# Two output units of a scan-and-matmul kernel summed in two pieces: six tiles' shares in step 24, shelved in SBUF, and joined by VectorE in step 26

## What is computed

```
decay = exp(-exp(w)) * (0.5 + 0.5 * tf)          # tf = sigmoid(sum(time_emb)), one per batch
ek = exp(min(k, 30)); ekv = ek * v               # here k = v = fside
nf, df = forward scans of ekv, ek with decay     # a = a * decay + x, over 1024 times
nb, db = the same, backward
num = nf + nb - ekv + exp(min(u + k, 30)) * v
den = df + db - ek  + exp(min(u + k, 30))
base = sigmoid(x) * num / max(den, 1e-8) * (0.8 + 0.2 * tf)
out = x + base @ (sign(weight) * mean|weight|).T + bias
```

## Time and profile before

| | |
|---|---|
| median of 3 runs | 514.49 us (511.86 to 514.51) |
| the profiled execution's own time | 513.52 us |
| its span in the trace | 511.5 us |
| VectorE busy | 482.0 us (94%) |
| ScalarE, GpSimd, TensorE busy | 413.9 (81%), 380.3 (74%), 352.3 us (69%) |
| mean granted TensorE clock | 0.87 |

### The profile page before, as it was taken

One profiled execution on the slowest core, in us unless ns is written; L12 is line 12 of the kernel. 1 busy time (PEld: TensorE's weight loads), 2 busy tenths in 40 slices (PEclk: granted clock), 3 DMA queues, 4 the chain that ended last, 5 costly groups with the idle time before them and its releaser, 6 DMA issues.

```text
span 511.5 us, 5395 instructions
## 1 busy us (share of the span) xinstructions
PE 352.3 (69%) x1797; PEld 206.7 (40%) x1803; DVE 482.0 (94%) x346; ACT 413.9 (81%) x461; POOL 380.3 (74%) x210
## 2 busy tenths in 40 slices
PE   3323223332194877878597879869739999999996
PEld 2213223332152444335354445535425555544442
DVE  6999999999999699999999999999999999999566
ACT  3979899899979889988987989998797888894500
POOL 0067778748764987789788687889897799899483
PEclk9997666565678798898987989989987999999999
DMA  8878999999987498798979869989792679975379
GB/s 219 220 220 267 263 260 243 307 297 251 246 191 179 68 240 182 163 199 189 195 170 160 201 130 203 197 178 202 162 162 49 118 124 157 178 127 80 42 107 223
DMA packets 101283, 94.22 MB, mean 184 GB/s; under 512 B 2924, under 2 KB 93064, under 8 KB 100744
## 3 DMA queue, kind: packets, MB, share of 16 engines
q0 software_dynamic: 31440, 36.18, 46.9%
q1 hardware_dynamic: 67720, 56.65, 35.7%
q10 hardware_dynamic: 2096, 1.05, 0.8%
HBM read 60.31 MB, written 37.75 MB: 192 GB/s over the span
## 4 chain that ended last, share of the span: by engine, by line
POOL 27%; ACT 25%; PE 21%; issue 18%; DVE 7%; DMA 0%; SPq 0%; ACTq 0%; DVEq 0%; POOLq 0%
POOL wkv L379 11%; PE prod L447 8%; POOL acts L342 5%; POOL out_dram L355 4%; ACT x_nat L801 4%; POOL wkv L385 3%; ACT euk L659 3%; PE prod L488 3%; ACT terms L655 3%; ACT L806 3%; POOL terms L388 2%; ACT L801 2%; ACT rec L690 2%; PE sT L488 2%; PE kT L488 2%
## 5 line engine op out<-in xcount | busy, mean ns | idle before, releaser
L447 PE MATMUL prod<-acts,sgn 128*128 128x512 f16 x752 | 182.7, 399 | 0.0
L925 DVE TENSOR_TENSOR_SCAN terms<-cols,y_start,terms 128x1024 f32<-128x1024 f32 x64 | 147.0, 2337 | 1.1
L911 DVE TENSOR_TENSOR_SCAN terms<-cols,terms 128x1024 f32<-128x1024 f32 x64 | 142.8, 2272 | 0.0
L362 POOL TENSOR_TENSOR wkv<-wkv,terms 128x1024 f32<-128x1024 f32 x31 | 73.5, 2370 | 54.8 <-DVE wkv L954 54.8
L447 PEld LDWEIGHTS prod<-acts,sgn 128*128 128x128 f16 x752 | 77.2, 103 | 88.5 <-issue 16.7
L379 POOL TENSOR_TENSOR wkv<-euk,rec 128x1024 f32<-128x1024 f32 x31 | 82.1, 2648 | 33.2 <-ACT rec L692 33.1
L342 POOL TENSOR_TENSOR acts<-wkv,rec 128x1024 f16<-128x1024 f32 x30 | 78.4, 2612 | 5.0 <-ACT rec L701 4.9
L385 POOL TENSOR_TENSOR wkv<-wkv,rec 128x1024 f32<-128x1024 f32 x31 | 79.6, 2569 | 1.2 <-ACT wkv L753 1.2
L422 PE MATMUL prod<-ident,o_nat 128*128 128x128 f16 x64 | 8.3, 311 | 72.0 <-ACT o_nat L794 72.0
L422 PE MATMUL sT<-ident,x_nat 128*128 128x128 f32 x208 | 36.7, 334 | 27.5 <-ACT x_nat L801 11.2
L422 PE MATMUL kT<-ident,k_nat 128*128 128x128 f32 x248 | 43.4, 333 | 15.9 <-DVE own L942 15.8
(11 more groups left out here) (120 smaller groups left out, 585.7 us busy)
## 6 DMA issues: line engine op xcount, KB each, us to landing
terms<-own POOLq DMA_DIRECT2D x32, 512.0 KB, 5.2
out_dram<-in_x_dram SPq DMA_DIRECT2D x32, 512.0 KB, 7.2
k_nat<-in_fside_BxSxS_dram SPq DMA_DIRECT2D x30, 512.0 KB, 6.4
x_nat<-in_x_dram SPq DMA_DIRECT2D x26, 512.0 KB, 4.9
out_dram<-o_nat POOLq DMA_DIRECT2D x24, 512.0 KB, 8.4
y_fm<-in_L_ffn_weight_dram SPq DMA_DIRECT2D x8, 512.0 KB, 8.4
out_dram<-in_L_ffn_bias_dram POOLq DMA_DIRECT2D x8, 512.0 KB, 6.6
x_end<-in_x_dram SPq DMA_DIRECT2D x6, 512.0 KB, 8.7
```

Of the source, the lines that this page charges most:

```text
L362: pool.tensor_tensor(wkv[n % 2][:, :], wkv[n % 2][:, :], ekv[n % NV], ALU.mult).then_inc(st["base"], 1)
L447: ins = pe.matmul(made_in(u), view[:, c, m % CT * P:m % CT * P + P], acts[:, part, m // CT % 2 * CT + c, h * H:(h + 1) * H], start=(part = ...
L911: dve.tensor_tensor_scan(buf, d, buf, 0.0, ALU.mult, ALU.add).then_inc(st["F" + kind], 1)
L925: dve.tensor_tensor_scan(buf[:, ::-1], d, buf[:, ::-1], y_start[:, i:i + 1], ALU.mult, ALU.add)\
```

## The change

Units 35 and 36 are summed in two pieces. In step 24 TensorE first sums the shares of tiles 16 to 21 of both (12 matmuls each, `begun`); ScalarE empties them with scale and bias onto two shelves in SBUF (`shelve`, at the end of exps(25)), and only then does TensorE start units 33 and 34 in the same banks (`shelved`). In steps 25 and 26 units 35 and 36 take the 4 matmuls of tiles 22 and 23 alone, ScalarE's evac(35) and evac(36) go, and VectorE joins bank and shelf into y_fm, both after `own` of step 26 (`fused`). Besides, in step 25 halves(23) come ahead of inverse(24) on ScalarE, and lo(23) ahead of the store and of chk(24) on GpSimd.

```diff
+    SHELVED = (4 * CT + 3, 4 * CT + 4)
+        shelf = [acts[:, 0, 2 * CT - 2 + i, :].bitcast(F32) for i in range(len(SHELVED))]
# GpSimd, step
                 if low:
                     base(n - 2)
+                if n == LAST + 1:
+                    low_half(n - 2, p)
                 if n < N - 1:
                     for m in ready[0:1]:
                         store(m)
...
-                if low:
+                if low and n != LAST + 1:
                     low_half(n - 2, p)
# TensorE
+            def emptied(u):
+                if u in SHELVED:
+                    pe.wait_ge(st["fused"], SHELVED.index(u) + 1)
+                else:
+                    done(pe, "ev", u - sum(v < u for v in SHELVED))
+            def shelve(u):
+                done(pe, "lo", u // (2 * CT) * CT + CT - 3)
+                product(u, range(CT - 2), 0, CT - 3).then_inc(st["begun"], 1)
             def unit(u):
                 done(pe, "lo", u // (2 * CT) * CT + CT - 1)
-                done(pe, "ev", u - 2)
-                product(u, range(CT)).then_inc(st["prod"], 1)
+                emptied(u - 2)
+                if u in SHELVED:
+                    product(u, range(CT - 2, CT), CT - 2).then_inc(st["prod"], 1)
+                else:
+                    product(u, range(CT)).then_inc(st["prod"], 1)
                 if ahead:
                     turned(made(n) - 1)
-                    for u in (made(n) + 1, made(n) + 2):
+                    for u in SHELVED:
+                        shelve(u)
+                    for i, u in enumerate((made(n) + 1, made(n) + 2)):
+                        pe.wait_ge(st["shelved"], i + 1)
                         part(u, 0, CT - 2)
# ScalarE
+            def shelve(i):
+                m = SHELVED[i] // 2
+                act.wait_ge(st["begun"], i + 1)
+                act.activation(shelf[i], made_in(SHELVED[i]), ACT.Identity, scale=oscale[:, m:m + 1],
+                               bias=bcol[:, m:m + 1]).then_inc(st["shelved"], 1)
             def clear(lo, hi):
                 for u in range(lo, hi):
-                    evac(u)
+                    if u not in SHELVED:
+                        evac(u)
             def step(n, p, wt, nxt, nxt3, mid, low, late):
+                if n == LAST + 1:
+                    done(act, "base", n - 2)
+                    halves(n - 2, p)
                 if mid:
                     inverse(n - 1, 1 - p)
...
-                if low and not hasty:
+                if low and not hasty and n != LAST + 1:
...
                     exps(n + 1, 1 - p)
+                if n == LAST:
+                    for i in range(len(SHELVED)):
+                        shelve(i)
# VectorE, after own(n)
+                if n == LAST + 2:
+                    for i, u in enumerate(SHELVED):
+                        done(dve, "prod", u)
+                        done(dve, "yT", u - 4)
+                        dve.scalar_tensor_tensor(y_fm[u // 2 % 2][:, u % 2 * H:(u % 2 + 1) * H], made_in(u),
+                                                 oscale[:, u // 2:u // 2 + 1], shelf[i], ALU.mult, ALU.add)\
+                           .then_inc(st["fused"], 1)
```

More of the change, by code:

```diff
@@ L183, in bi_wkv_binary_ffn @@
             "ln", "rec", "chk", "two", "inv", "gate", "base", "hi", "hib", "lo",
-            "prod", "ev", "yT", "yc", "abs", "sgn", "wT", "wTc", "orow", "orow_sb", "early", "early_sb", "soon", "nat", "weighed", "joined", "scaled", "whole",
+            "prod", "ev", "yT", "yc", "abs", "sgn", "wT", "wTc", "orow", "orow_sb", "early", "early_sb", "soon", "begun", "shelved", "fused", "nat", "weighed", "joined", "scaled", "whole",
             "res", "prior_hi", "prior_hib", "prior_lo", "last_den", "last_ln", "last_rec", "last_chk", "last_inv", "last_gate",
@@ L440, in s_turn, with product @@
                      ident[:, :]).then_inc(st["sT"], 1)
-            def product(u, tiles):
+            def emptied(u):
[3 more added lines that the diff above has]
+                    done(pe, "ev", u - sum(v < u for v in SHELVED))
+            def product(u, tiles, opens=0, closes=CT - 1):
                 m, h = u // 2, u % 2
@@ L448, in product @@
                                         acts[:, part, m // CT % 2 * CT + c, h * H:(h + 1) * H],
-                                        start=(part == 0 and c == 0), stop=(part == 1 and c == CT - 1))
+                                        start=(part == 0 and c == opens), stop=(part == 1 and c == closes))
                 return ins
+            def shelve(u):
+                done(pe, "lo", u // (2 * CT) * CT + CT - 3)
+                product(u, range(CT - 2), 0, CT - 3).then_inc(st["begun"], 1)
             def part(u, lo, hi):
@@ L464, in unit @@
                 done(pe, "lo", u // (2 * CT) * CT + CT - 1)
-                done(pe, "ev", u - 2)
-                product(u, range(CT)).then_inc(st["prod"], 1)
+                emptied(u - 2)
[3 more added lines that the diff above has]
+                    product(u, range(CT)).then_inc(st["prod"], 1)
             def turned(u):
                 if 0 <= u < 2 * LAST:
-                    done(pe, "ev", u)
+                    emptied(u)
                     done(pe, "yc", u - 1)
@@ L510, in step @@
                 if n == N - 2:
-                    done(pe, "ev", 2 * LAST - 2)
+                    emptied(2 * LAST - 2)
                     begun(0)
@@ L544, in step @@
                 if first and n != LAST + 1:
-                    done(pe, "ev", units[0] - 2)
+                    emptied(units[0] - 2)
                     part(units[0], 0, CT - 1)
@@ L559, in step @@
                 if first and n != LAST + 1:
-                    done(pe, "ev", units[1] - 2)
+                    emptied(units[1] - 2)
                     part(units[1], 0, CT - 1)
```

## The result

| | before | after |
|---|---|---|
| median | 513.73 us (4 runs, 511.86 to 514.51) | 519.59 us (4 runs, 518.74 to 520.86) |
| profiled execution, its span | 513.52 us, 511.5 us | 518.78 us, 516.9 us |

The changed kernel is slower: ratio of the times 1.0122, 95% interval 1.0081 to 1.0162. The forecast was 520.1 us.

The account below looks back on a forecast made before the run. The prediction took VectorE to bound the kernel: 7.9 us of later scans, joins included, less 1.3 us of overlap given back, made 6.6 us on the profiled 513.52, so 520.1 us, with a range of 516.5 to 522.4 us.

Parts of the forecast that it names:

- VectorE bounds: Whole kernel: VectorE, busy 94% of the span, sets the time; the end moves one for one with its shift at gate(28).
- Rival (c): TensorE's backlog from 386 us on sets the end, so 24 fewer matmuls there give 508.3 us; chance 0.06.
- the wait of 0.59 us: Step 30, at 457.04: TensorE's wait for a ScalarE copy ahead of the tail, taken as its backlog's slack of 0.59 us.
- Part 1: The two joins on VectorE: about 0.65 us each, together a cost of 1.3 us.
- Part 2: Shelving in step 24: 24 matmuls, 5.2 us, cost nothing on TensorE; two evacuations put ScalarE 1.3 us later.
- Part 3: Step 25's new order: two(24) 5.1 us later (halves 1.2, lo 2.3, store 1.6); gate(24) waits 2.4 us for inv(24).
- Part 4: Joins' inputs: TensorE idles 6.4 us before turned(32), half clock follows, join 36 waits, step 26's scans begin 7.9 us late.
- Rival (a): Step 25: same mechanism, but TensorE's clock stays up or returns at once; scans 4.9 us late, 517.1 us; chance 0.18.
- Part 5: Step 27: the overlap of inv(26) with den(27) is gone, giving back 1.34 us on VectorE.
- Sum: Whole kernel: 7.9 - 1.3 = 6.6 us on the profiled 513.52, forecast 520.1 us; chance 0.56.

Follow-up runs that it names:

- e4: The kernel before with 24 matmuls (tiles 16 to 21 of units 35 and 36) left out and nothing in their place: 511.37 us, ratio 0.9989.
- e1: The changed kernel with step 25 in its old order, shelving and joins alone: 515.0 us, ratio 1.0051.
- e3: The changed kernel with the store's DMA issue in step 25 back ahead of lo(23): 517.92 us, ratio 1.0104.
- e6: The changed kernel with both joins behind the forward scans of step 26 instead of ahead of them: 515.07 us, ratio 1.005.
- e12: The changed kernel with TensorE repeating tile 24's transposes 5 times ahead of turned(32): 516.34 us, ratio 1.0091.
- e11: The changed kernel with TensorE repeating tile 24's transposes 4 times ahead of turned(32): 516.88 us, ratio 1.0091.
- e10: The changed kernel with TensorE repeating tile 24's transposes 3 times ahead of turned(32): 519.2 us, ratio 1.012.
- e9: The kernel before with two more 128x512 passes on VectorE in step 28, results unused: 513.81 us, ratio 1.0031.
- e5: The changed kernel with TensorE repeating tile 24's transposes 6 times ahead of turned(32): 516.52 us, ratio 1.0079.
- e2: The kernel before with the new order of step 25 alone, no shelving and no joins: 518.06 us, ratio 1.0108.

## Why the prediction was right, point by point

**VectorE bounds, and its shift at step 28 is the shift of the end.** Right for the changed kernel. Between den(28) and the last VectorE instruction lie 79.55 us before and 79.51 after, though TensorE had 24 matmuls less behind it and waits 2.00 us once in step 30. e4, with less work on TensorE alone, keeps the distance as well (79.53). Rival (c) is out: what e4 takes off TensorE doesn't come back at the end. It isn't a law, though: in e1 and e3 the clock fell in step 30, the wait of 0.59 us was used up, and the end came 0.9 us later than VectorE's shift.

**Part 1, joins 1.3 us.** 1.32 in e1, 1.33 in e6.

**Part 2, the shelving.** Right: it is free on TensorE, which waited 1.29 us for the first shelving and still ended its sums at 382.9. On ScalarE the first pass behind the table load starts at 375.91; with the 1.19 us by which den(25) stood earlier in this execution that is 377.1, as forecast, 1.3 us behind the 375.77 of the earlier trace rows. This 1.3 us isn't free: it is a part of the 5.1 us of part 3, and in e1, without the new order, it brings inv(24) beside den(25).

**Part 3.** two(24) stands 0.18 us behind den(25)'s start, before 4.95 ahead of it: 5.13 us later, forecast 5.1. gate(24) waits 2.46, forecast 2.4. The store's share of the 5.1, put at 1.6, is 1.54 by e3.

**Part 4.** TensorE idles 6.49 us (6.4), half clock follows, the scans begin 7.79 us late (7.9). The second join waits 2.85 us, a little less than the 3 to 4 that I gave; the first waits 0.88, which the forecast's own numbers had (own ends at 392.5, join 35 at 393.3) and which costs nothing of its own, as the second waits for the same engine behind it. Rival (a) is the one whose size was off: I priced a clock that stays up at 3.0 us less, e12 and e11 show 2.4. From turned(32) to the end of unit 36 I had walked 3.6 us at the full clock, and the second join came 4.0 us behind it; at half clock I had walked 6.6, and it was 6.46. The walk at the full clock already had the second join waiting 1.05 us (393.15 to 394.2); it waits 1.35.
The Trainium skill, "TensorE: Matmul & The Clock Gate", "What's actually happening", has the clock low when the engine has idled; the changed kernel and e10 agree (0.50 behind breaks of 6.49 and 4.20 us).

**Part 5.** den(27) takes 1.23 us, 1.33 less than in the earlier trace rows, and the loss falls from 7.79 to 6.46. From there to the tail nothing on VectorE waits for over 0.2 us.

**Sum.** Forecast 6.6, found 6.46. The profiled executions differ by 5.26 us only, since den(25) stood 1.19 us earlier in the one after: 6.46 - 1.19 = 5.27. That is scatter and no part of the change: e9, whose code up to step 28 is that of before, has den(25) at 384.89. The medians differ by 5.86. That the time itself came within 0.5 us, 519.59 against 520.1, is in part luck: the four runs of the changed kernel lie 2.1 us apart, and the one execution on which the forecast was built turned out to lie 0.2 us from the median of before.

## What to carry to other kernels

Ask of the engine that seems full whether a wait still stands ahead of the work that sets the end; here it did (0.59 us), and 5.2 us of matmuls moved away from TensorE could bring 1.3 us at most, which the two joins put back on the engine that does bound. Before one instruction goes ahead in an in-order queue, walk everything that it pushes back, DMA issues included, to the bounding engine: 1.2 us of halves that came later, 2.3 us of lo(23) and 1.5 us of a store became 5.1 us at two(24) and, by a second path over an evacuation and TensorE, 6.5 us on VectorE. A consumer placed on the bounding engine costs its wait too, so it goes where its input is long there: behind two scans the same joins cost 3.6 us less.

## What the runs showed beyond that

**TensorE's clock after a break.** The break's length alone doesn't tell whether the clock falls. Ahead of turned(32) 1.33 us (e1), 2.14 (e12) and 3.03 (e11) left it at 1.00, 4.20 (e10), 4.96 (e3) and 6.49 didn't. In step 30, behind the same matmuls, a break of 2.02 us was followed by half clock in e1 and e3; one of 2.02 us in e5 and e10, and one of 2.00 us in the changed kernel, was not. The break and the work behind it, e1 first:

```profile
450.42:452.44 2.02, 0.00 (x0) 0.00 (x1) 1.88 (x3) 1.58 (x3) 2.02 (x2) 1.00 1.33 167
452.44:455.44 3.00, 3.00 (x8) 1.12 (x9) 3.00 (x2) 2.91 (x4) 3.00 (x4) 0.57 0.05 6
```

```profile
456.04:458.04 2.00, 0.00 (x0) 0.00 (x1) 1.86 (x3) 1.58 (x3) 2.00 (x2) 1.00 1.39 175
458.04:462.20 4.16, 3.63 (x16) 1.48 (x16) 4.13 (x3) 4.07 (x6) 4.16 (x4) 1.00 0.06 9
```

e1 and e3 are also the two kernels that need 0.9 us more from den(28) to the end (80.46 and 80.44 against 79.5 in all others): the 8 matmuls behind the break took 3.21 us in e1, 2.98 in e3 and 1.90 in the changed kernel. In e1 the next 15 then begin 29.43 us behind den(28) and without a wait (457.59), in the changed kernel 28.47 us behind it and after the wait of 0.59 (462.26). What decides between the two cases wasn't tried, and stays open; whether the other runs of e1 and e3 had the low clock there isn't known, as one execution of each was profiled.

**VectorE beside GpSimd.** A den that starts while GpSimd's product runs can take longer, and then ends 1.1 us after it: 2.09 us in e1, 3.23 in e3 (inv(24) ends at 388.01, den(25) at 389.10), 2.56 before; 1.23 in e4, where GpSimd's product had started 2.86 us ahead and was over. Where the den starts first GpSimd's product can take longer instead (2.90 us in e2, 0.53 us behind den(25)). The Trainium skill, "SBUF — State Buffer", "Who interferes with whom", tells of a pair of ports that these two engines share under an exclusive lock; the durations here agree.

Such overlaps come and go between executions, and they make the scatter of den(25). Take from its start what the 25 dens ahead of it took over 1.22 us each and what VectorE waited, and 363.0 us are left in every one of the 13 profiled executions, within 0.2, while the starts lie up to 3.5 us apart. Between before and after, the dens account for 1.09 and the waits for 0.13 of the 1.19 us; most of it is two dens, at 313 us (2.52 and 1.67 us) and at 164 us (2.03 and 1.78).
